# One edge column of every 11th group fetched row by row by the sync engine instead of gathered by GpSimd, in three passes of a graph network on one core

## The reference

```python
msg = x[src] * edge_weight[:, None]                  # layer 0: weighted mean, two products, rows normalised
msg = relu(x[src] + edge_attr)                       # layer 1: sum over dst, then a two-layer MLP
msg = concat([x_i, x_j - x_i]) @ W.T + b             # layer 2: sum over dst, batch norm, leaky relu
# layer 3: eight relations; attention softmax over the edges of each dst, per relation
x = _layernorm(x + layer(x))                         # after each
```

## Time and profile before

| | |
|---|---|
| time, median of 3 runs | 8350.87 us (8347.98 to 8354.85) |
| profiled execution | 8359.45 us, its span 8357.6 us |
| GpSimd busy | 6047.8 us (72%) |
| TensorE busy | 3610.3 us (43%) |
| VectorE busy | 3081.2 us (37%) |
| gathers | 6272, of them 4704 in passes 0 to 2 |
| packets of the sync engine's queue (q1) | 345920, 271.71 MB |

### The profile page before, as it was taken

The page is one execution under the profiler, slowest core; times in us unless marked ns, Lnnn a source line. Parts: engine busy times, 40 slices in busy tenths (PEclk is TensorE's granted clock), DMA queues, the critical chain, the costliest instruction groups (busy, mean ns, idle before and its releaser), DMA issues.

```text
span 8357.6 us, 58639 instructions
## 1 busy us (share of the span) xinstructions
PE 3610.3 (43%) x14426; PEld 2863.1 (34%) x14427; DVE 3081.2 (37%) x5673; ACT 992.2 (12%) x3180; POOL 6047.8 (72%) x6306
## 2 busy tenths in 40 slices
PE   3434343433343444444343444343532555555555
PEld 2333333333222222222222222222322445545555
DVE  3323232223223232223222222222343566667666
ACT  0000000000000000000000000000121233433333
POOL 7777777776777777777677777777447777777771
PEclk6555656556565565656565656665665666566666
DMA  2111111111222222222111111111254455555553
GB/s 58 30 30 30 30 30 30 29 31 40 55 56 55 56 56 56 55 56 54 27 28 29 28 29 28 29 28 29 73 168 102 121 141 132 139 137 137 139 136 94
DMA packets 575347, 546.50 MB, mean 65 GB/s; under 512 B 344667, under 2 KB 344667, under 8 KB 575008
## 3 DMA queue, kind: packets, MB, share of 16 engines
q0 software_dynamic: 200704, 212.34, 13.8%
q1 hardware_dynamic: 345920, 271.71, 11.6%
q10 hardware_dynamic: 28384, 58.61, 2.3%
HBM read 440.61 MB, written 100.74 MB: 65 GB/s over the span
## 4 chain that ended last, share of the span: by engine, by line
POOL 72%; issue 26%; PE 1%; DVE 1%; DMA 0%; POOLq 0%; ACT 0%; DVEq 0%; ACTq 0%; SPq 0%
POOL gat L774 72%; PE p_b L1421 1%; DVE oh L1701 0%; DMA spare<-rel_d 0%; POOLq L282 0%; DVE work L2185 0%; ACT msg L1025 0%; PE p_a L1451 0%; POOL spare L827 0%; DVE sum_t L2084 0%; PE p_a L1482 0%; PE p_a L1480 0%; DMA gat<-rel_d,idx 0%; PE p_a L1427 0%; DVE dtab L2129 0%
## 5 line engine op out<-in xcount | busy, mean ns | idle before, releaser
L774 POOL DMA_INDIRECT gat<-x_d,idx x3136 | 2984.7, 952 | 1012.6 <-issue 955.4
L774 POOL DMA_INDIRECT gat<-rel_d,idx x1568 | 1545.6, 986 | 641.3 <-issue 477.8
L774 POOL DMA_INDIRECT gat<-in_x,idx x1568 | 1491.8, 951 | 485.9 <-issue 477.7
L1285 PE MATMUL p_all<-oh,gat 128*128 128x256 f32 x1568 | 716.9, 636 | 1195.0 <-DMA gat<-x_d,idx 1174.8
L1285 PE MATMUL p_all<-oh,msg 128*128 128x256 f32 x1568 | 720.6, 640 | 1177.4 <-DVE oh L1701 822.3
L1271 PE MATMUL p_all<-oh,msg 128*66 128x128 f32 x3136 | 704.2, 418 | 1193.5 <-DVE oh L1701 1193.5
L1701 DVE SCALAR_TENSOR_TENSOR oh<-dstf,fine_col,p_b 128x512 f32<-128x512 f32 x1578 | 1105.2, 741 | 108.4 <-DVE sum_t L1800 92.3
L1271 PEld LDWEIGHTS p_all<-oh,msg 128*66 128x66 f32 x3136 | 638.4, 231 | 1256.0 <-DVE msg L1827 1237.2
L1285 PEld LDWEIGHTS p_all<-oh,gat 128*128 128x128 f32 x1568 | 484.0, 323 | 1424.4 <-DMA gat<-x_d,idx 1321.9
L1285 PEld LDWEIGHTS p_all<-oh,msg 128*128 128x128 f32 x1568 | 490.0, 328 | 1400.4 <-ACT msg L928 1295.7
L1800 DVE TENSOR_TENSOR sum_t<-sum_t,p_all 64x128 f32 x784 | 222.5, 284 | 1435.3 <-PE p_all L1285 1275.5
(11 more groups left out here) (277 smaller groups left out, 3461.4 us busy)
## 6 DMA issues: line engine op xcount, KB each, us to landing
he_d<-gat ACTq DMA_DIRECT2D x196, 288.0 KB
ea<-he_d SPq DMA_DIRECT2D x196, 288.0 KB
ea<-in_edge_attr SPq DMA_DIRECT2D x196, 256.0 KB, 2.7
gat<-x_d,idx POOLq DMA_INDIRECT x3136
drow<-dst_d SPq DMA_DIRECT2D x196, 256.0 KB, 3.5
spare<-rel_d SPq DMA_DIRECT2D x98, 288.0 KB, 4.0
gat<-in_x,idx POOLq DMA_INDIRECT x1568
gat<-rel_d,idx POOLq DMA_INDIRECT x1568
```

Source lines behind the costliest of these rows:

```text
L774: nc.gpsimd.indirect_dma_start(out=gat[:, q, s, :] if width == HROW else got[:, q, s, :], out_offset=None, in_=table, in_offset=bass.Indir ...
L1285: ins = nc.tensor.matmul(p_sum[:, c % 2, 0:2 * W], rows_of(s), oh[:, c % 2, s:s + 2, :].rearrange("p s w -> p (s w)"), start=(s == 0), sto ...
```

## The change

In passes 0 to 2, every 11th group from group 16 on (16, 27, ..., 192: 17 groups, "lent") gets its last column, s = 7, from SP. GpSimd issues seven gathers there. During the 11 steps ahead of a lent group SP fetches its 128 rows one by one into `side`, a pair of buffers in a part of `trip` that is free in these passes: at each step it loads 8 or 12 source numbers from SBUF into registers, and for each issues a transfer of one row of 64 floats whose source address is a register. The numbers come from a new input, `src_l` (17 x 128), loaded once. At the lent group's own step SP waits until the slot is free and until all 128 rows have landed, and copies the column from `side` into slot q. The users of the group wait for `s_gat[q]` with its new count and also for `s_lent`. Pass 3 keeps eight gathers in each group; the waits are counted anew. Some semaphores of a branch that isn't taken for sorted edges now share names.

```diff
+SPREAD = 11
+LENT = range(SPREAD + Q + 1, G, SPREAD)
...
+        side = part_of(trip, 2 * T, 2, D)
+        side_i = trip[0:len(LENT), 2 * T + 2 * D:2 * T + 2 * D + P].bitcast(i32)
...
+        def lands(n, t):
+
+            gathers = lambda upto: sum(S - (g in LENT) for g in range(t % Q, upto, Q))
+            return 16 * (gathers(t + 1) + n * gathers(G) if n < 3 else 3 * gathers(G) + S * (t // Q + 1))
+
+        def landed_rows(eng, n, t):
+
+            eng.wait_ge(s_gat[t % Q], lands(n, t))
+            if t in LENT:
+                eng.wait_ge(s_lent, 16 * (n * len(LENT) + LENT.index(t) + 1))
...
             sp.wait_ge(s_prep, 3)
+            sp.dma_start(side_i, src_l).then_inc(s_load[1], 16)
...
+            def lent_rows(n, t):
+
+                for k, to in enumerate(LENT):
+                    if not to - SPREAD <= t < to:
+                        continue
+                    if n == 0 and k == 0 and t == to - SPREAD:
+                        sp.wait_ge(s_load[1], 32)
+                    lo, hi = [4 * (P // 4 * (t - to + SPREAD + j) // SPREAD) for j in range(2)]
+                    _, row_of = nc.values_load_multi_w_load_instructions(
+                        side_i[k:k + 1, lo:hi], engines=[sp.engine], min_val=0, max_val=N - 1,
+                        skip_runtime_bounds_check_because="a source is the number of a node")
+                    for p, v in zip(range(lo, hi), row_of):
+                        sp.dma_start(side[p:p + 1, k % 2, :], X[n][bass.ds(v, 1), :]).then_inc(s_side[k % 4], 16)
+
+            def lent_column(n, t):
+
+                if t in LENT:
+                    k, q = LENT.index(t), t % Q
+                    turns = len(range(k % 4, len(LENT), 4))
+                    sp.wait_ge(s_free[q], t // Q + 1 + IT * n)
+                    sp.wait_ge(s_side[k % 4], 16 * P * (turns * n + k // 4 + 1))
+                    sp.dma_start(got[:, q, S - 1, :], side[:, k % 2, :]).then_inc(s_lent, 16)
+
...
                     if Q <= c < 2 * BODY:
+                        lent_column(n, it * BODY + c)
+                        lent_rows(n, it * BODY + c)
+                    if Q <= c < 2 * BODY:
                         t = it * BODY + c
-                        wait_for(sp, s_gat[q], it * (128 * BODY // Q) + 128 * (c // Q + IT * n))
+                        sp.wait_ge(s_gat[q], lands(n, it * BODY + c - Q))
...
-                def group(q):
-                    for s in range(S):
+                def group(q, lent=False):
+                    for s in range(S - 1 if lent else S):
...
-                        group(q)
+                        group(q, not looped and width == D and it * Q + q in LENT)
...
-                    wait_for(dve, s_gat[q], it * (128 * BODY // Q) + 128 * (c // Q + 1))
+                    landed_rows(dve, 0, t)
...
-                    wait_for(dve, s_gat[q], it * (128 * BODY // Q) + 128 * (c // Q + 1 + IT))
+                    landed_rows(dve, 1, it * BODY + c)
```

More of the change, by code:

```diff
@@ L46, with program @@
            ("att", (64, 16)), ("rbias", (1, 512))]
-def program(nc, x, src_p, dst_p, type_p, weight_p, dst_f, type_f, dst_c, dst_w, type_w, edge_attr, weights, out):
+def program(nc, x, src_p, src_l, dst_p, type_p, weight_p, dst_f, type_f, dst_c, dst_w, type_w, edge_attr, weights, out):
     f32, i32, i16, bf16 = mybir.dt.float32, mybir.dt.int32, mybir.dt.int16, mybir.dt.bfloat16
@@ L206, in program @@
         s_pre, s_msg = sem("s_pre"), sem("s_msg")
+        s_side, s_lent = [sem(f"s_side{k}") for k in range(4)], sem("s_lent")
         s_oh = {n: [sem(f"s_oh{n}_{h}") for h in range(1 if n == 3 else 2)] for n in (0, 1, 2, 3, 5)}
@@ L217, in program @@
         s_again, s_again_exp = sem("s_again"), sem("s_again_exp")
-        s_any_dma, s_any_in, s_any_used = sem("s_any_dma"), sem("s_any_in"), sem("s_any_used")
+        s_any_dma, s_any_in = sem("s_any_dma"), sem("s_any_in")
         s_any_acc, s_any_sum = sem("s_any_acc"), sem("s_any_sum")
-        s_any_gap, s_any_exp = [[sem(f"s_any_{n}{k}") for k in range(2)] for n in ("gap", "exp")]
+        s_any_gap, s_any_exp, s_any_used = s_side[0:2], s_side[2:4], s_lent
         NS = 6
@@ L242, in program @@
         s_turn = sem("s_turn")
-        every_pass = [*s_idx, *s_gat, *s_free, *s_ea, *s_hest, *s_held, s_pre, s_msg, *s_oh[0], *s_oh[1], *s_oh[2],
+        every_pass = [*s_side, s_lent, *s_idx, *s_gat, *s_free, *s_ea, *s_hest, *s_held, s_pre, s_msg, *s_oh[0], *s_oh[1], *s_oh[2],
                       *s_oh[3], *s_oh[5], *s_agg, *s_sum.values(), s_scan_copy, *s_drow, s_drused, s_shifted,
@@ L656, in feed @@
                 if lo + Q < G:
-                    wait_for(sp, s_gat[i % Q], it * (128 * BODY // Q) + 128 * (i // Q + 1 + 3 * IT))
+                    sp.wait_ge(s_gat[i % Q], lands(3, t))
                     sp.dma_start(idx[:, i % Q, :], key_d[:, bass.ds(t + Q, 1), :].rearrange("p a s -> p (a s)"))\
@@ L1008, in landed @@
                 q, t = i % Q, it * BODY + i
-                wait_for(act, s_gat[q], it * (128 * BODY // Q) + 128 * (i // Q + 1 + 3 * IT))
+                act.wait_ge(s_gat[q], lands(3, t))
                 nc.scalar.activation(score[0:P, bass.ds(t + 1, 1), 0, :].rearrange("p a s -> p (a s)"),
@@ L1263, in add_up @@
                 t = it * BODY + c
[L1264 to L1267, removed]
+                wait_for(pe, s_msg, t + (1 + G * n))
                 for s in range(S):
@@ L1280, in add_up_pairs @@
                 else:
-                    wait_for(pe, s_gat[c % Q], it * (128 * BODY // Q) + 128 * (c // Q + 1 + 2 * IT))
+                    landed_rows(pe, n, t)
                 for s in range(0, S, 2):
@@ L2507 @@
     }
-    args = [given("x", np.pad(i["x"], [(0, NP - N), (0, 0)])), given("src_p", grouped(src)), given("dst_p", grouped(dst)),
+    args = [given("x", np.pad(i["x"], [(0, NP - N), (0, 0)])), given("src_p", grouped(src)),
+            given("src_l", src.reshape(G, P, S)[list(LENT), :, S - 1]), given("dst_p", grouped(dst)),
             given("type_p", grouped(kind)), given("weight_p", grouped(padded(i["edge_weight"]))),
```

## The result

The changed kernel takes 8284.7 us (median, 8281.75 to 8286.61), the kernel before in the same runs 8349.85 (8347.98 to 8354.85): a ratio of 0.9921, with a 95% interval of 0.9908 to 0.9934, and 65.1 us less. The prediction said 8287, with a sum of 64.0 us.

A forecast was written before the change was run, and what follows sets the result against it. The prediction took GpSimd's fixed-pitch gathers as the bound: 17 x 1.2526 + 17 x 1.2596 + 17 x 1.2517 = 64.0 us saved, SP's added work hidden, so the median goes from 8350.87 to 8286.9 us, range 8282 to 8326.

The forecast's parts named there:

- GpSimd bounds, and a gather is worth its pitch: Passes 0 to 2: each of 51 gathers removed saves its whole pitch, about 1.25 us, 64.0 us in all.
- The rows lie in SP's idle time: SP's step in passes 0 to 2: 8.15 us (8.52 in pass 1) fits under GpSimd's 9.9, costing nothing.
- the signs named: What the profile after should show if the forecast held: gather count, pitch, pass lengths, SP's row and load times, no column waits.
- the 28.9 us after pass 0: Time from the last gather of pass 0 to the start of pass 1, expected to stay as before.
- The load: Row numbers into SP's registers each step: twelve in one instruction taken at 1.10 us, between 0.30 and 3.65.
- The new waits: SP's wait at the column delays an index fetch 8 to 10 us, with 26 us left; VectorE's and TensorE's waits empty.
- the forecast margin of 1.4 to 1.75 us a step: Time by which SP's step was expected to stay shorter than GpSimd's in passes 0 to 2.
- Rival 1: SP's step in passes 0 to 2 becomes the bound, loads paid per register: 365 us lost, 8652 us; chance 0.10.
- Rival 2: Remaining gathers slow beside the new transfers, 0.0079 us on each of 4653: 37 us back, 8324 us; chance 0.08.
- Rival 3: The lent column, not GpSimd, lets the group be used; nothing gained, 8351 us; chance 0.05.
- Rival 4: SP's fetched rows land one behind another at 2.5 us each: 10.8 ms more; chance 0.01.
- The sum against its execution: Whole kernel: 64.0 us off the profiled 8359.45 gives 8295.5; off the median 8350.87 it gives 8286.9.

The follow-up runs named there:

- run 1: The changed kernel without SP's row-number loads, row fetches, column copies and their waits; lent groups keep seven gathers: 8284.21 us, ratio 0.9926 to the kernel before.
- run 2: The changed kernel with eight gathers in every group again; SP still fetches all 6528 rows but copies no column: 8346.94 us, ratio 0.9999 to the kernel before.
- run 6: The changed kernel with every 8th or every 6th group lent instead of every 11th: 8253.18 us (ratio 0.9885) and 9024.66 us (1.0807) against the kernel before.
- run 3: The kernel before, with no edit, profiled once more: one run, 8338.92 us.
- run 4: The changed kernel with every 7th group lent instead of every 11th, and six row semaphores for four: 8296.2 us, ratio 0.9937 to the kernel before.

## Why the prediction was right, point by point

- **GpSimd bounds, and a gather is worth its pitch.** Right, and shown by runs 1 and 2: 64.0 us expected, 65.1 measured, 63.4 without SP's work (8347.58 - 8284.21).
- **The rows lie in SP's idle time.** Right, but the terms were too high. A row was put at 0.57 us and takes 0.41: the register operation takes 0.037 us where 0.053 was taken, a MOVE of 0.029 that the program's order does not show comes with each row, and the transfer holds SP for 0.23 us, below the lower bound of 0.33 that the trace gave. The one-row loads at the start were the nearest in shape and not in cost. The step is 0.36 (index fetch) + 1.17 (to the first row, with the load of 0.95) + 4.80 = 6.3 us (1029.73 to 1036.06) in place of 8.15. Of the signs named, rows at 0.5 to 0.6 us and a load of 1 to 2 us did not come, because both are cheaper; the pitch within 0.005 us and the 28.9 us after pass 0 did (29.8 us from the last gather's start to the next in place of 29.9).
- **The load.** 1.10 was taken; the median is 0.95 where nearly all loads are of twelve registers, and 1.19 for sixteen (run 6): 0.06 us for each register more. The margin was larger than forecast, not nearly gone. The Trainium skill (Runtime: NRT & Kernel Launch, section Instruction fetch mechanics) gives about 200 ns per register, and speaks there of the register loads that the runtime puts into a program. For these loads from SBUF that figure does not hold, and the measurement decides.
- **The new waits.** Right. SP waits at the column for the freed slot and makes the lag good in two or three steps; with the forecast margin of 1.4 to 1.75 us a step, 8 to 10 us would have taken five to seven. Nobody waits for the column.
- **Rival 1, SP as the bound.** It has the right mechanism at another place: it comes with every 7th group (in pass 1) and with every 6th (in all three), as more rows fall on a step. What brought it were more rows a step, at 0.41 us each with 0.06 for the load of its number, not a load paid at 0.304 us a register.
- **Rival 2, slower gathers.** Fell at its size of 37 us with runs 1 and 2: the 6528 transfers alone change the time by no more than some 8 us. Its 0.0079 us is the difference in pitch between passes 1 and 2, which the changed kernel keeps (1.2580 against 1.2500); what makes it was not tested.
- **Rivals 3 and 4.** Fell with the list of waits: no wait for the column, and at the column SP waits for the slot, not for the rows.
- **The sum against its execution.** The working took 8295.5 for the profiled execution; the profile of after lies at 8283.96, 75.5 us lower and not 64. That is the difference between two executions (run 3), and the forecast was rightly made for the median.

## What to carry to other kernels

Where one engine issues work of a fixed pitch and sets the time, each item moved to an idle issuer is worth one pitch, until the idle issuer's own step is as long. So size the other engine's step first, in rows of its own timeline with the gaps between instructions, and leave a margin: from every 8th to every 7th group the same idea goes from 95 us gained to 51, and at every 6th it loses 676. The version with every 8th group (8253.18 us) and that with every 7th and the attribute loads on ScalarE (8251.19) beat both kernels here.

## What the runs showed of the hardware that was not expected

A transfer of one row of 256 bytes whose address is in a register holds SP for 0.228 us, less than one of 128 rows with a fixed address (0.328 in the kernel before), and twelve of them in 4.8 us do not slow the gathers beyond run 2's interval. The gather's pitch differs from execution to execution of one kernel by 0.0017 to 0.0035 us in 1.25 (run 3). Most of it is not in a few long gathers: in passes 0 to 2 the median gather takes 947 ns in the first profile of before and in that of run 1, and 944 in the other eight. The profiles of runs 1 to 4 come from the same chip, so it is not a matter of the chip alone; what sets it stays open, and no run was made for it. Over 4704 gathers it is 8 to 16 us, about what the runs of one kernel differ by (8337.37 to 8354.57).
